# Layer 2's feedforward gets a new table of steps in a four-layer decoder kernel, and the output jobs of layer 3's attention are packed two to a step

## The reference: four layers, of which two matter here

```python
# layer 2, feedforward: the weights are rounded to -1, 0, 1 times a mean,
# the activations to 8 bits with the maximum of each token
x = x + bitlinear(layernorm(gelu(bitlinear(layernorm(_layernorm(x)), w1, b1))), w2, b2)   # 128 -> 512 -> 128
# layer 3, attention: 16 heads of 64 columns, 256 keys, softmax, then Wo (1024 -> 128)
x = x + L3_attn(_layernorm(x))
# layer 3, cross attention inside each token: 16 heads of 8 columns, each attends to the 16 heads
energy = einsum('nhld,ngld->nlhg', q, k);  attn = softmax(energy / sqrt(128))
out = einsum('nlhg,ngld->nhld', attn, v);  x = x + layernorm(out) @ Wo.T + bo
```

## Time and profile before

| | us |
|---|---|
| median of 3 runs | 1128.22 |
| lowest, highest | 1125.24, 1134.36 |
| the profiled execution | 1124.19 |
| its span, first to last instruction | 1122.3 |
| TensorE busy | 822.0 (73%) |
| VectorE busy | 611.0 (54%) |
| ScalarE busy | 349.2 (31%) |
| GpSimd busy | 316.3 (28%) |

### The profile page before, as it was taken

One profiled execution on the slowest core, in us unless ns is written; L12 is line 12 of the kernel. 1 busy time (PEld: TensorE's weight loads), 2 busy tenths in 40 slices (PEclk: granted clock), 3 DMA queues, 4 the chain that ended last, 5 costly groups with the idle time before them and its releaser, 6 DMA issues. The chain is left out here.

```text
span 1122.3 us, 15955 instructions
## 1 busy us (share of the span) xinstructions
PE 822.0 (73%) x5961; PEld 597.9 (53%) x5969; DVE 611.0 (54%) x1414; ACT 349.2 (31%) x683; POOL 316.3 (28%) x318
## 2 busy tenths in 40 slices
PE   4974896974657185579887764999999896257994
PEld 2542453573434073367754432677877686135984
DVE  2644862313299952486565787855335337942221
ACT  1110475330112111125544560454343232111331
POOL 1344100203148724122221111000034045615222
PEclk9985798895678677689998895999999998568998
DMA  9302200450000004325365000000000000005674
GB/s 370 135 2 84 70 5 1 126 166 18 20 0 1 0 1 92 87 52 119 72 165 158 4 1 1 1 2 1 1 2 1 1 1 1 0 1 198 216 265 141
DMA packets 44678, 72.44 MB, mean 65 GB/s; under 512 B 4817, under 2 KB 36737, under 8 KB 43033
## 3 DMA queue, kind: packets, MB, share of 16 engines
q1 hardware_dynamic: 38921, 65.72, 19.7%
q0 software_dynamic: 1728, 3.59, 0.9%
q10 hardware_dynamic: 3952, 2.10, 0.7%
HBM read 58.65 MB, written 15.89 MB: 66 GB/s over the span
## 5 line engine op out<-in xcount | busy, mean ns | idle before, releaser
L847 DVE TENSOR_REDUCE space<-PS 128x2 f32<-128x512 f32 x128 | 83.2, 686 | 40.1 <-PE PS L651 39.9
L2545 DVE TENSOR_REDUCE space<-PS 128x2 f32<-128x512 f32 x64 | 43.3, 689 | 80.5 <-PE PS L2242 80.3
L831 ACT ACTIVATE annex<-PS 128x384 f32<-128x384 f32 (+1 forms) x128 | 67.2, 544 | 58.2 <-PE PS L662 29.1
L2261 PE MATMUL PS<-space 64*128 64x256 f32 x256 | 68.0, 411 | 4.6 <-issue 4.6
L2281 PEld LDWEIGHTS PS<-space 128*128 128x128 f32 x512 | 61.7, 193 | 17.4 <-issue 16.5
L2281 PE MATMUL PS<-space 128*128 128x65 f32 x512 | 69.1, 282 | 0.2 <-ACT space L2363 0.2
L1950 POOL TENSOR_TENSOR space<-space 128x1536 f32<-128x1536 f32 x16 | 54.6, 3437 | 38.3 <-DVE space L1881 32.1
L1170 PE MATMUL PS<-space 128*128 128x128 f32 x444 | 57.1, 284 | 7.9 <-DVE space L1305 5.0
L2242 PE MATMUL PS<-space 64*128 64x256 f32 x256 | 62.7, 401 | 0.1
L1305 DVE TENSOR_TENSOR space<-PS,space 128x512 f32<-128x512 f32 (+1 forms) x28 | 19.2, 687 | 75.8 <-ACT space L1232 70.6
L1170 PEld LDWEIGHTS PS<-space 128*128 128x128 f32 x444 | 53.3, 197 | 10.9 <-DVE space L1305 6.0
(11 more groups left out here) (492 smaller groups left out, 2209.9 us busy)
## 6 DMA issues: line engine op xcount, KB each, us to landing
space<-in_e_l_ffn SPq DMA_DIRECT2D x22, 768.0 KB, 5.3
space<-in_e_l_ffn SPq DMA_DIRECT2D x23, 192.0 KB, 3.0
l_ffn_sorted<-in_slots SPq DMA_DIRECT2D x2, 1584.0 KB, 25.6
space<-l_attn_scratch_k SPq DMA_DIRECT2D x8, 384.0 KB
space<-l_ffn_sorted SPq DMA_DIRECT2D x10, 264.0 KB, 4.4
weights<-in_w_l_xattn SPq DMA_DIRECT2D x1, 2504.0 KB, 15.2
weights<-in_w_l_attn SPq DMA_DIRECT2D x1, 2124.0 KB, 11.9
space<-l_xattn_scratch_q SPq DMA_DIRECT2D x4, 512.0 KB, 3.5
```

The lines of the kernel that those rows point to most:

```text
L831: nc.scalar.activation(P[:, u % 8, 0:keys], PS[:, 3 + u % 2, 0:keys], ACT.Exp).then_inc(exp_done, 1)
L847: nc.vector.tensor_reduce(m[:, :, at_h], max_bank(u).rearrange("p (c k) -> p c k", c=2), AX_X, ALU.max).then_inc(max_done, 1)
L2261: nc.tensor.matmul(out, kk[:, 128 * kc:128 * kc + 128], q, start=True, stop=False)
L2545: nc.vector.tensor_reduce(MX[:, b % 2, :, h], PS[:, max_bank[a], :].rearrange("p (c k) -> p c k", c=2), AX_X, ALU.max).then_inc(max_done, 1)
```

## The change

Two tables of numbers and one constant are changed. No instruction is added or removed; TensorE, VectorE and ScalarE get another order, GpSimd in a few small instructions of the pieces, SP none.

```diff
-SHIFT = 176
+SHIFT = 170
...
-    PLAN = {"in": (-58, -42, -24, -9), "twice": (-54, -38, -20, -6), "norm1": (-50, -34, -16, -2), "quant1": (-49, -33, -11, -1),
-            "f1": (-43, -26, -6, 4), "f2": (-36, -23, -3, 7), "gelu": (-33, -21, -2, 8), "hidden": (-29, -17, 1, 11), "norm2": (-24, -12, 4, 14),
...
+    PLAN = {"in": (-52, -30, -5, 8), "twice": (-49, -26, -3, 10), "norm1": (-46, -21, -1, 13), "quant1": (-45, -20, 1, 14),
+            "f1": (-38, -16, 3, 15), "f2": (-32, -13, 4, 17), "gelu": (-30, -11, 6, 18), "hidden": (-27, -8, 8, 19), "norm2": (-24, -5, 10, 21),
+            "affine2": (-23, -4, 11, 22), "quant2": (-22, -3, 12, 23), "f3": (-17, 0, 14, 25), "f4": (-15, 1, 15, 26), "attn": (-14, 2, 16, 27),
+            "normed": (-11, 4, 17, 28), "T": (-9, 5, 18, 29)}
...
-            place(second_at(16 * b + 15) + 4 + i + i // 3, ("t", "t", "o")[i % 3], b, i)
+            place(second_at(16 * b + 15) + (3, 3, 4, 4, 5, 6)[i], ("t", "t", "o")[i % 3], b, i)
```

## The result

The changed kernel takes **1156.64 us** (median of four runs, 1146.52 to 1168.6) against 1127.26 for the kernel before in the same session: a ratio of 1.0238, 95% interval 1.0194 to 1.0283. The ratio leaves out runs in a slower state (of the changed kernel the one of 1168.6, at a mean clock of 0.816), so that it gives a loss of 26.8 us where the medians give 29.4. The forecast was 1126 with a range up to 1139. The profiled execution took 1155.26, its span is 1153.4 (before 1122.3), and TensorE is busy 851.4 us (822.0) with the same instructions, at a mean clock of 0.831 (0.854).

What follows compares the result with a forecast made beforehand. VectorE was taken to bound the stretch before the first maxima, TensorE the middle, VectorE and GpSimd the tail. Terms 0.6 + 3.5 + 4.6 + 1.1 + 1.0 = +10.8, with -13.2 give -2.4: 1128.2 to 1126, range 1111 to 1139.

Steps and rivals of the forecast that it cites:

- Part 1: Up to the first maxima: VectorE loses 16.0 us of work ahead of `normed`; first maxima at 691.5, 12.2 us earlier.
- Part 2, the turns at full clock: Steps 0 to 19: engines take turns, first eight steps walked at 24.1 us; all 12 us gone, net 0.6 lost.
- The clock term: Steps 0 to 5: TensorE's pauses may lower its clock; ends 0 and 6.7 us, 3.5 taken.
- Part 3: The middle: jobs moved ahead 4.6, lost pause cover 1.1, output transposes 1.0; E, the last weighted values' end, moves +10.8.
- The upper end: 6.7 us for the clock: doubled TensorE work in steps 0 to 5 delays the 16th maxima 6.1, the rest 0.6.
- The 4.5 us wait: Step 14: `f3` waits 4.5 us for `quant2` of sequence 2, which ends at 732.2.
- Rival 2: From 693 to 745: TensorE stays at 1.2 GHz through the first scores, +12.8, 1141; mean clock under about 0.65; chance 0.12.
- the 4.6: The middle: sequence 2's last output job, `xk`, `xv` and `xT` now stand ahead of E, 4.6 us.
- the 0.24 under "Numbers": Chance of faster by over 1% (under 1117): 0.7 of rival 1 and 0.04 of the forecast.
- Part 4: The tail behind E: first product at E+1.9, shift at E+11.0 against E+24.2 before; -13.2 us.
- "After it both orders are the same": Behind the shift in the tail: new and old order the same, so no further gain or loss.
- the collision: Tail: `normedo` may be held up 4.1 us by GpSimd's product if GpSimd starts first; +1.5 net.

Runs made afterwards that it cites:

- number 13: Changed kernel with extra unused matmuls in all score waits and the last maxima's pause, GpSimd's product waiting for sequence 3's `normedx`: 1127.61 us, ratio 1.0000.
- number 6: Changed kernel with six extra unused matmuls in the 5.71 us pause ahead of unit 48's second scores, nothing else: 1145.38 us, ratio 1.0154.
- number 11: Kernel before with five extra unused matmuls in its own 4.63 us pause ahead of unit 48, nothing else: 1126.75 us, ratio 1.0005.
- number 2: Kernel before with only layer 3's attention output jobs packed into steps 3, 3, 4, 4, 5, 6: 1132.31 us, ratio 1.0063.
- number 1: Changed kernel with its new table, but layer 3's attention output jobs at their old steps: 1148.44 us, ratio 1.0202 against the kernel before.
- number 9: Changed kernel with a table in which TensorE's jobs follow the VectorE pieces they need by more steps: 1145.31 us, ratio 1.0123.
- number 5: Changed kernel with extra unused matmuls in six score waits, fewer than first tried and in the other auxiliary bank: 1151.45 us, ratio 1.0233.
- numbers 3: Changed kernel with extra unused matmuls ahead of six waiting score jobs, in those jobs' own bank: 1155.15 us, ratio 1.023.
- number 7: Changed kernel where GpSimd's product of sequence 2's values also waits for sequence 3's `normedx` on VectorE: 1153.54 us, ratio 1.0265.
- number 10: Changed kernel with the later table of number 9, six extra matmuls in unit 48's pause, and GpSimd's wait for `normedx`: 1129.61 us, ratio 1.0025.
- number 12: The kernel of number 10 with extra unused matmuls also in the remaining score waits, in a bank nothing holds: 1126.07 us, ratio 0.9966.

## Why the prediction was wrong, step by step

**Part 1** was right: `normed` at 674.5 (673.4), first maxima at 692.6 (691.5).

**Part 2, the turns at full clock**, was nearly right. Each named wait is there: 4.23 ahead of `f4`, 3.83 ahead of `f1`, 3.29 ahead of `T`, 4.11 ahead of step 14's `f3` (forecast 4.5), 1.43 ahead of `f1` (2.5). The walk gave 24.1 us for the first eight steps; number 13, where the clock held, took 24.9. From the first maxima to step 20 it gave 63.0, some 64 to unit 28's maxima, and number 13 took 69.4, of which some 3 us go to the 6.8 us at half (an estimate: the two jobs in them took 3.72 us, against 1.95 at full clock). So the early start is paid back even at full clock, as forecast; but the whole was to be 5.9 us faster at full clock (-2.4 - 3.5), and number 13 is level.

**The clock term is the step that failed.** The mechanism was named, the size was not: the prediction gave it two ends, 0 and 6.7, took 3.5 for the scores, and put nothing for the pause of the last maxima (Part 3). The runs showed 13.9 us that number 13 gave back in the scores, and 9.9 that number 6 gave back behind the pause. The upper end came from the first eight steps alone: there it was right (723.5 - 692.6 = 30.9 us, and 24.1 + 6.1 = 30.2). But I ended the sum where the first waits ended. The 4.5 us wait that I had put into step 14 calls up a stretch of its own. Behind that wait TensorE waits for 2 us in 33, so there is hardly any slack to hide a slow clock. Units 22 to 28 took 31.7 us (before 15.0), and 24.5 in number 13 with 6.8 still at half; the clock is thus 7.2 us of it at least, some 10 with what was left at half, and the rest goes with the new order, which has two more of the `q` and `k` jobs in this place (3.72 us at half). The Trainium skill ("TensorE: Matmul & The Clock Gate", Terms), by which a throttled stretch costs half its length, gives as an estimate 25.6 us for the 51.2 us at half in the scores. That is more than the some 17 us of number 13 (13.9 and what was left in it), as it is for the first stretch alone (10.2 by the rule, 6.0 measured), where VectorE covers part, but nearer than my 3.5. Behind the pause it gives 12.0 for the change (9.9 measured) and 1.7 for the kernel before (1.7 measured, number 11). I had set it against my walk for the first stretch and kept the walk.

**Rival 2** named the mechanism and had 0.12. Its place was wrong: the mean clock from 693 to 745 was 0.78, above its 0.65, and steps 8 to 13 ran at full clock. It too looked for one stretch.

**Part 3.** The cover of the pause (`xw`) was costed as idle time, 1.1 us. The pause did grow from 4.63 to 5.71, and unit 63 to E grew by 10.2 us with it, against 1.1 forecast; number 6 gave 9.9 back. The packing alone (number 2) made it 4.2 longer with the same pause, the table alone (number 1) 0.1: the size of the loss needs both, and why is open. The row that spoke of it was at hand: in the earlier trace rows the first four L2261 behind the pause take 1.18 us, against 0.71 for four at full clock (at 899.37 in the same trace), so the clock was already down there. The jobs moved ahead cost 4.3 (5.6 forecast, 3.6 without the jobs that stand ahead of unit 28). The terms of the 4.6 in it add up to 4.9, and the 0.24 under "Numbers" is 0.22 by its own terms; neither changes anything here.

**Part 4** gave -13.2, and -4.0 came: 4.3 us for a later shift, 4.8 behind it. First product at E+1.3 (E+1.9). The shift came at E+15.3, not E+11.0: VectorE waits 5.07 us for the last output product (L2202). With the clock at 1.00 there it was 13.7 (number 2), so the walk of the output jobs was some 2.7 us short and the clock took the rest. "After it both orders are the same" was wrong: same order on each engine, but a race between two. I had looked for the collision at `normedo`, which took 0.59; it was at `normedx`, where both engines became ready within 0.01 us. The Trainium skill ("SBUF — State Buffer", "Who interferes with whom") says that the first one holds the port for its whole instruction, and 5.71 beside 5.37 agrees. So does the other place that I had named by it, the splitting of the last maxima. It took 0.18 us before, and now, beside a product of GpSimd that ends at 909.09, 2.69:

```profile
900.12 8.97 POOL L2607 TENSOR_TENSOR weights<-CTX,annex 128x2048 f32<-128x2048 f32 x2 [7.26 <-ACT CTX L2341]
```
```profile
906.43 2.69 DVE L2551 TENSOR_SCALAR space<-space 128x32 bf16<-128x32 f32 x1
```

It was covered, as forecast: `M` follows on TensorE at 913.32 without a wait.

## What to carry to other kernels

A pause on TensorE has two prices, its own length and the clock behind it (here 1.1 us more of pause and 9 us behind it), and the second falls on work that has no slack. Before you take cover away from a pause, or put a product one step behind the piece that it needs, look at the clock column behind the pauses that are there already. To tell clock from order, put matmuls whose results nobody uses into the wait, in a bank that is free when the wait begins: if the order were at fault nothing would change. When a table moves work out of a stretch, measure past the place where the work went (number 9: 21.4 us gained at unit 28, 12.8 at unit 63). And where two engines that hold each other up start within 0.1 us, a reordering elsewhere can turn who is first.

## What the runs showed of the hardware

- The length at half clock behind a pause is not set by the pause alone. Behind 4.63 us it was 3.4 us (before) and 6.8 (number 1), behind 5.71 it was 10.2 (number 2), 13.7 (number 5) and 23.9 (the change, numbers 3, 7 and 9), in one profiled execution each. What decides between these is open.
- The clock also fell without a long wait: in number 10 the clock fell at 749.4 behind waits of 0.78 and 1.38 us, and stayed down for 10.2 us of unbroken work. With three extra matmuls in these two waits (number 12) it did not fall.
- Not everything collides: VectorE's L2474, with one of its two inputs in PSUM, took its 2.23 us beside GpSimd's 5.46 (number 7), while L2379 was held up for 5.1 us beside GpSimd's 5.37 in the change.
